# Image additions as accumulating transfers, norm sums in passes of their own, setup beside the first sample: a fused convolution, filter and scan kernel on one Trainium2 core

## The reference

```
h = x + conv3x3(relu(mask(groupnorm(x))))          # the mask depends on each channel's centre of mass
h = h + filter1(groupnorm(h))                      # 2x up by a 12-tap filter, leaky relu, clip, 2x down
g = groupnorm(h)                                   # input of the scan block
x', z = split(in_w @ g)                            # 1x1 convolution, 128 + 128 channels
f1, f2, f3 = 1x1 conv of x', then two 2x2 stride-2 convs   # levels of 784, 196 and 49 pixels
y  = selective scans with 16 states over f3, f2, f1 (both directions), layer norm of each, upsampled and added
h = h + out_w @ (y * silu(z))                      # x3 in the kernel
out = h + filter2(groupnorm(h))
```

## Time and profile before

| | |
|---|---|
| median of 3 runs | 6593.88 us (6589.45 to 6598.32) |
| profiled execution, its own time | 6592.31 us |
| its span, first to last instruction | 6590.5 us |
| PE busy | 5872.6 us (89%) |
| DVE busy | 5785.4 us (88%) |
| ACT busy | 4123.9 us (63%) |
| POOL busy | 269.1 us (4%) |
| mean granted TensorE clock | 0.935 of full |

### The profile page before, as it was taken

One profiled execution on the slowest core, in us unless ns is written; L12 is line 12 of the kernel. 1 busy time (PEld: TensorE's weight loads), 2 busy tenths in 40 slices (PEclk: granted clock), 3 DMA queues, 4 the chain that ended last, 5 costly groups with the idle time before them and its releaser, 6 DMA issues. The chain is left out here.

```text
span 6590.5 us, 87758 instructions
## 1 busy us (share of the span) xinstructions
PE 5872.6 (89%) x32460; PEld 3815.8 (58%) x32460; DVE 5785.4 (88%) x4685; ACT 4123.9 (63%) x8002; POOL 269.1 (4%) x69
## 2 busy tenths in 40 slices
PE   5779999999999999999999999999999989999956
PEld 3445656655656655656655656655556655666634
DVE  1798889989899988989989899989899989899984
ACT  2556666666666666666666666666666666676654
POOL 0000000000000000000000000000000000000000
PEclk9889999999999999999999999999999999999978
DMA  1333323333333333323333333333333333333331
GB/s 41 92 92 85 102 81 105 98 86 89 96 86 105 98 83 92 99 82 106 98 82 93 95 88 105 98 85 90 97 87 104 98 87 88 101 85 102 98 83 41
DMA packets 332919, 597.12 MB, mean 91 GB/s; under 512 B 105718, under 2 KB 174526, under 8 KB 332362
## 3 DMA queue, kind: packets, MB, share of 16 engines
q1 hardware_dynamic: 332492, 591.50, 33.9%
HBM read 294.91 MB, written 58.81 MB: 54 GB/s over the span
## 5 line engine op out<-in xcount | busy, mean ns | idle before, releaser
L1209 DVE TENSOR_TENSOR_SCAN hb<-da,hb 128x1570 f32<-128x1570 f32 (+2 forms) x704 | 2332.7, 3343 | 6.1 <-ACT da L1020 2.2
L641 PE MATMUL ps<-pad,conv_w 128*128 128x392 f32 x4608 | 1563.9, 493 | 0.0
L641 PEld LDWEIGHTS ps<-pad,conv_w 128*128 128x128 f32 x4608 | 870.2, 189 | 660.7 <-issue 42.7
L691 PEld LDWEIGHTS ps<-down_k,ys 121*128 121x128 f32 x9216 | 1108.2, 193 | 205.7 <-DVE ys L1085 120.5
L691 PE MATMUL ps<-down_k,ys 121*128 121x121 f32 (+1 forms) x9216 | 1137.7, 276 | 83.0 <-DVE ys L1085 82.9
L672 PE MATMUL ps<-xt,up_k 123*121 123x256 f32 (+2 forms) x4096 | 1149.2, 426 | 6.6 <-ACT ys L920 6.3
L1224 DVE TENSOR_TENSOR hb<-hb,c_t 128x3136 f32<-128x3136 f32 (+1 forms) x384 | 1150.0, 3008 | 1.3
L1025 ACT ACTIVATE da<-delta_t,a_neg 128x784 f32<-128x784 f32 x1024 | 912.8, 940 | 316.3 <-DVE hb L1209 312.9
L1192 DVE TENSOR_TENSOR hb<-dx_t,b_t 128x3136 f32<-128x3136 f32 x256 | 880.4, 3439 | 49.6 <-PE ps L778 47.0
L920 ACT ACTIVATE ys<-ps 121x512 f32<-121x512 f32 x1152 | 670.2, 590 | 376.1 <-PE ps L672 246.6
L672 PEld LDWEIGHTS ps<-xt,up_k 123*121 123x121 f32 x4096 | 660.5, 192 | 330.3 <-ACT ys L920 159.8
(11 more groups left out here) (136 smaller groups left out, 5771.1 us busy)
## 6 DMA issues: line engine op xcount, KB each, us to landing
dx_t<-vc SPq DMA_DIRECT2D x256, 392.0 KB, 6.4
b_t<-scr SPq DMA_DIRECT2D x256, 392.0 KB, 4.1
delta_t<-vd SPq DMA_DIRECT2D x256, 392.0 KB, 6.9
c_t<-scr SPq DMA_DIRECT2D x256, 392.0 KB, 4.3
xa<-in_x SPq DMA_DIRECT2D x32, 784.0 KB, 4.4
xs<-xa SPq DMA_DIRECT2D x32, 784.0 KB, 3.3
xb<-xs SPq DMA_DIRECT2D x32, 784.0 KB, 5.5
out<-xb SPq DMA_DIRECT2D x32, 784.0 KB, 7.8
```

The source lines that it names most:

```text
L641: mm = nc.tensor.matmul(ps[:, half, 0:HALF], conv_w[:, c, tap, m * P:(m + 1) * P], pad[:, c, r0:r0 + HH // 2, tap % 3:tap % 3 + WW], start ...
L691: mm = nc.tensor.matmul(img(ps[:, reg, 0:17 * WW])[:, h + h0:h + h1, w + w0:w + w1], ys[0:KP, y % NY, at + n * P:at + (n + 1) * P], down_k ...
L1209: nc.vector.tensor_tensor_scan(h, a, b, 0.0, ALU.mult, ALU.add).then_inc(scan_done, 1)
```

## The change

Both identity matmuls are gone. `ca` and `x3` write what PSUM holds plus the bias, and POOL then issues a transfer that adds the image to it in SBUF: `ax.m` adds the input image, read again from HBM, to `xa`; `ay.m` adds the spilled image to `xb`. The step `back` falls away. Since the copies no longer see the finished image, norms 2 and 1 get `gp` passes on ACT, in place, which wait for the transfers. The projections of the last two scan branches (`bc.2` and `bc.3`) become one matmul pair, with one copy and one write. The setup block is gone: the first image is loaded first of all, constants in two lists after it, and the products that build the filter matrices stand on DVE just ahead of the first `clip`. All five tables are new, and a sample's filter 2 and last scan steps stand up to one pass earlier.

```diff
@@ conv
-                    if n == 0:
-                        nc.tensor.matmul(ps[:, half, 0:HALF], ident[:, :], xa[:, m, half * HALF:(half + 1) * HALF], start=True, stop=False)
...
-                                              start=False, stop=(i == NC * TAPS - 1))
+                                              start=(i == 0), stop=(i == NC * TAPS - 1))
@@ bo
-                    pe.wait_ge(x_back, 16 * (s + 1))
                     for half in range(2):
-                        nc.tensor.matmul(out[:, half, 0:HALF], ident[:, :], xb[:, m, half * HALF:(half + 1) * HALF], start=True, stop=False)
...
@@ gp
-                    spare_free(s, k, c)
-                    nc.scalar.activation(spare(k, c), image(k, c), ACT.Identity, accum_out=gsum[k][:, 0, c:c + 1]).then_inc(gn_act[k], 1)
+                    if k == FIRST_GN:
+                        act.wait_ge(x_added[c], 16 * (s + 1))
+                    if k == LAST_GN:
+                        act.wait_ge(x2_added[c], 16 * (s + 1))
+                    out = image(k, c)
+                    if k == B_GN:
+                        spare_free(s, k, c)
+                        out = spare(k, c)
+                    nc.scalar.activation(out, image(k, c), ACT.Identity, accum_out=gsum[k][:, c:c + 1]).then_inc(gn_act[k], 1)
@@ ca
-                    nc.scalar.activation(xa[:, m, half * HALF:(half + 1) * HALF], ps[:, half, 0:HALF], ACT.Identity, bias=conv_b[:, m:m + 1],
-                                         accum_out=gsum[FIRST_GN][:, half, m:m + 1]).then_inc(conv_added, 1)
+                    nc.scalar.activation(xa[:, m, half * HALF:(half + 1) * HALF], ps[:, half, 0:HALF], ACT.Identity,
+                                         bias=conv_b[:, m:m + 1]).then_inc(conv_added, 1)
@@ gpsimd
+                def ax(s, m):
+                    pool.wait_ge(conv_added, 4 * s + 2 * m + 2)
+                    pool.dma_start(xa[:, m, :], sample(t["x"], s)[:, m, :], accum_op=ALU.add).then_inc(x_added[m], 16)
+                def ay(s, m):
+                    pool.wait_ge(x3_done, 2 * s + m + 1)
+                    pool.wait_ge(x_spilled, 16 * (s + 1))
+                    pool.dma_start(xb[:, m, :], xs[s][:, m, :], accum_op=ALU.add).then_inc(x2_added[m], 16)
@@ sync, ahead of the table
+                sp.dma_start(xa[:, :, :], sample(t["x"], 0)).then_inc(x_loaded, 16)
+                for dst, src in early:
+                    sp.dma_start(dst, src).then_inc(s_early, 16)
...
@@ clip
+                    if y == 0:
+                        weights()
@@ tables
-zm@1 zc@0
+zm@1 ax.0@0 ax.1@0 zc@0 ay.0@1 ay.1@1
```

More of the change, by code:

```diff
@@ L86 @@
+bl.6@2 cl.4@2 bl.7@2 cl.5@2 xl.3.3@2 xl.3.1@2 xl.3.2@2 xl.3.0@2 dl.3.1@2 dl.3.0@2 dl.3.2@2 dl.3.3@2 cl.6@2 bl.8@2
+cl.7@2 spill@1 load@0 bl.9@2 bcw.0@1 bcw.1@1 cl.9@2 cl.8@2 bcw.2@1 dl.0.2@1 bl.1@1 xl.0.2@1 bl.0@1 cl.0@1 dl.1.3@1
+cl.1@1 xl.1.3@1 bl.2@1
 """
 PE_ORDER = """
-gm2.3@1 red.9@2 f1@1 f2@1 f3@1 bc.0@1 gm1.1@3 bc.1@1 gm1.0@0 bc.2@1 var.2@2 gm2.0@0 bc.3@1 z@1 red.10@2 gm2.1@3
-turn.0.0.0@3 turn.0.0.1@3 red.11@2 v.0@1 turn.0.0.2@3 turn.0.0.3@3 v.1@1 turn.0.1.0@3 up.0.0.0@3 up.0.0.1@3 up.0.0.2@3
@@ L230, in build @@
         F = [f1, f2, f3]
-        gsum = [sb(f"gsum{i}", [P, 2, NC]) for i in range(4)]
+        gsum = [sb(f"gsum{i}", [P, NC]) for i in range(4)]
         gsq = [sb(f"gsq{i}", [P, NC]) for i in range(4)]
@@ L739, in bc_of @@
                     lev, w = BRANCH[q]
+                    rows = 2 * N_STATE * (2 if q == 2 else 1)
                     out = take("bc", s, q)
                     pe.wait_ge(f_copied, 3 * s + lev + 1)
+                    weights = bc_w[:, w:w + (2 if q == 2 else 1), :].rearrange("p w r -> p (w r)")
                     for half, n in halves(LEN[lev]):
-                        mm = nc.tensor.matmul(out[0:2 * N_STATE, half, 0:n], bc_w[:, w, :], F[lev][:, half * HALF:half * HALF + n], start=True, stop=True)
+                        mm = nc.tensor.matmul(out[0:rows, half, 0:n], weights, F[lev][:, half * HALF:half * HALF + n], start=True, stop=True)
                     mm.then_inc(slot_full, 1)
@@ L998, in bce @@
                         act.wait_ge(scr_written, 16 * i)
-                    nc.scalar.copy(wide(bcr[0:2 * N_STATE, :], n), wide_ps(slot[0:2 * N_STATE, :, :], n)).then_inc(bc_copied, 1)
+                    nc.scalar.copy(wide(bcr[0:rows, :], n), wide_ps(slot[0:rows, :, :], n)).then_inc(bc_copied, 1)
                 def da_of(s, u, *p):
@@ L1262, in _ @@
                       "mix": mix, "gate": gate}
+                constants()
                 for kind, s, a in program(DVE_ORDER):
```

288 lines of the change are left out of this document (147 added, 141 removed).

## The result

The changed kernel takes 6234.5 us (median of 4 runs, 6221.8 to 6246.7) beside 6591.7 us for the kernel before (6588.4 to 6598.3): ratio 0.9457, interval 0.9431 to 0.9483. It is faster by 5.4%. The profiled execution takes 6223.9 us, with a span of 6222.1 us.

What follows compares the result with a forecast made beforehand. Bound: no single engine, but PE and DVE handing work over in a 197.6 us period. Sum: 6592.3 - 28 x (197.6 - 190) - 41 - 10 - 25 = 6303, given as 6305 us; range 6220 to 6400, wider 6180 to 6510.

Steps and rivals of the forecast that it cites:

- the start: Up to the first image's mask: image loaded ahead of the large weights, first sum at 12 us, saving 41 us.
- the fill: From the first mask until the fourth image's: 10 us off for PE's lighter passes.
- the end: After the last mask: 31 us less DVE work up to the gate, +6 net after it, so -25 us.
- PE's savings: Per image on PE: identity matmuls 6.9 us and halved wide `bc` matmuls 2.6 us, together 9.5 us less work.
- The new wait: Between convolution and filter 1's first transpose: a chain of 14.3 us, adding 6 us to PE's idle time.
- D: Time of the 392 KB accumulating transfer ahead of filter 1: taken as 7 us, entering one to one above that.
- The other moves: PE idle per period: -5 for clips and filter 2's norm, +3 ahead of `f1`, about -2.5 for slot waits.
- No bound by itself: Kernel before: DVE 180.1 and PE 182.0 us of work per 197.6 us period, handing over in turn; neither alone bounds it.
- The new order hands over no better: Rival: new waits use up PE's saving, period 196 to 198, only the ends pay, 6516 or 6475 us; chance 0.17.
- DVE becomes the bound: Rival: D of 3 to 4 and clips covered, period 183 to 186, 6152 us; chance 0.12.
- Slow transfers: Rival: held-up accumulating transfers, D of 17 us, period some 203, 6660 us; slower than before; chance 0.11.
- The rule against the change: DVE and POOL hinder each other; the skill warns GpSimd-issued transfers can be starved of descriptors and advises another queue.

Runs made afterwards that it cites:

- the old order with the new setup: Kernel before with only the new setup and the merged B/C product; its order, identity matmuls and sums in the copies stay: 6457.8 us, ratio 0.9794.
- The delayed transfer: Changed kernel with a plain 392 KB device-memory transfer issued and waited for on POOL ahead of `ax.1`: 6369.2 us, ratio 0.9656.
- the new order with matmuls: Changed kernel with both additions as identity matmuls again, sum passes kept, the copy loaded back by SP: 6819.4 us, ratio 1.0339.
- the run meant to tell it: Changed kernel with half of the reductions over the states left out for the two finest branches: 6222.0 us, ratio 0.9437.
- the old order with the transfers: Before's order tables with new setup, merged product, both additions as accumulating transfers and separate sum passes: 6958.4 us, ratio 1.0553.

## Why the prediction was right, and where it was off

The forecast was 6305 us with 6180 to 6510; measured were 6234.5. Against the profiled execution the sum of 6303 was 79 us too high. Term by term: the period 187.7 and not 190 (-66), the start as predicted (-41), the fill +8.6 and not -10 (+19), the end -57 and not -25 (-32).

- **PE's savings, 9.5 us.** The total is near: work fell by 10.5 us, to 171.5 where 172.5 was predicted. Its parts came out otherwise. The convolution's identity matmuls cost 2.4 us when they were put back, not 3.4. The wide `bc` matmuls fell from 144.3 to 42.9 us in the 28 periods, 3.6 us each and not 2.6, because they also run at a higher clock: 505 ns for a matmul of 392 columns, where the same merged pair takes 872 ns in the old order with the new setup.
- **Work into time.** The sum adds PE's work and PE's idle time, and takes it that work taken off shortens the period. The runs do not bear that out: 8.8 us less work on PE gave no time, and the 2.4 us put back cost 0.7. The period fell by as much as PE's work did (10.0 and 10.5 us) while DVE, with its work unchanged, idled 10 us less, and that came from the order. That the sum still fits is partly luck.
- **The new wait, chain 14.3 us, PE idle +6.** The place is right, the reason for the waiting only in part. D was 7 in the sum and is 4.9 us for the half that counts. The stretch is 13.2 us at full clock and 15.0 in the mean; with D = 4.9 the sum's own terms give 12.2. What makes it longer is not the transfer but PE's queue: the group mean stood behind one reduction and the transposes behind another and `v`, both slower at half clock, which the sum had at nothing. PE idles 4.8 us in the mean and not 6.5, half of it inside the layer norm. The delayed transfer agrees with D entering one to one in size, 4.2 us for 3.6.
- **The other moves.** -5 for the clips and filter 2's norm is -5.3 by the waits (2.2 and 3.1 us gone). +3 ahead of `f1` is a wait of 3.3 us there now, where the waits of before have 22.7/28 = 0.8. -2.5 for the slot waits around `f1`, `f2` and `z` is -1.5 (80.6 us in 28 images, now 38.1), and waits of 3.4 us inside the layer norm, 2.3 of them in the stretch above, were not seen. PE's idle time is 16.1 us where the sum had 17. With the 0.5 us by which 189.5 was rounded up and 1.0 us less work, this makes the 2.3 us by which the period was off. The addition to `xb` is hidden as predicted: ACT waited for it four times in 64.
- **What the prediction left out on DVE.** The softplus wait, which it said nothing addresses, fell by 3.5 us per image, and it stays in the old order with the new setup (108.9 us), so this is the order's doing. Against it stand 2.8 us for the scan factors. The late `da.2` that was feared is not where they arise in the image above: ACT ends its first part at 4901.44, and DVE works without a gap until its scan at 4904.97, so it has the slack of about 3 us that was predicted.
- **The start** was exact at 41 us: the first mask is at 23.2.
- **The fill** failed in its step "10 us off for PE's lighter passes". The old order with the new setup needs 498 us from the first mask to the fourth, the changed kernel 512, and the new order with matmuls 534. That points at the new order, whose fill the prediction did not count; which step does it was not followed up.
- **The end.** The step on the work from mask to gate gave 31 us and measured 40.5. The one that failed is "+6 net" after the gate: it is -16.4 (60.5 us for 76.9). What shortens that last filter was not tested.
- **No bound by itself.** The reading that two engines hand work to each other holds: DVE relieved by 12.3 us gives 1.2, PE relieved by 8.8 gives nothing, both together (12.3 and 11.7) 2.5. But the pair does not set the time by itself either, since both idle more in that last kernel. In the convolution VectorE is the bound. What sets the time in the other stages, PE's work or the round of waits over ACT, stays open: the run meant to tell it took no time off PE.
- **The rivals.** "The new order hands over no better" is out at 187.7 us. "DVE becomes the bound" came nearer than its chance of 0.12 said, with 7.4 us of idle time left, but DVE's own relief hardly shortens the period. "Slow transfers" needed D = 17; the slowest of 128 took 11.3 us. By the sum's own terms the first rival's 6475 at a period of 196 is 6471.
- **The rule against the change.** The row's side is seen again: beside POOL's multiplication three scans took 11.70 us, and 10.05 without it. Hold-ups of descriptors by whole scans do not show: DVE works through the second half's transfers as well, and they land within 4.7 to 5.3 us. The slow ones into `xa`, up to 11.3, are the first halves, beside other transfers. The Trainium skill (DMA: Bandwidth & Descriptors, section Anatomy of one DMA) would have given 2.9 us (an estimate from the page), and the sum near 6200 by it; the measurement, 4.9 us where the transfer is alone, is 1.7 times that, and it decides. That 6200 lies nearer to the result than 6305 is no support for the 2.9, since PE hardly waited for the transfer.

What the prediction did not see is how the parts depend on each other. It gave the transfers credit for PE's 6.9 us. In the runs, with the steps where they were put, the transfers in the old order cost 500 us (6958 beside 6458), the new order with matmuls is 585 us above the changed kernel, and only the two together gain 223 us over the new setup alone. The first transfer adds little to that.

## What to carry to other kernels

Moving an addition off TensorE changes when its operands are needed, and that can be worth more than the matmul time: here the output projection could move in front of a store and a reload. A change of operations and the order written for it have to be priced together, for each alone, as placed here, was slower than neither. And where in-order engines hand over in turn, taking work off one did not pay in a stage where another engine was the bound, so look at the busy time stage by stage before removing anything.

## What the runs showed of the hardware

- **Matmuls into four different groups of 32 output rows run side by side.** The reduction's eight matmuls of 392 columns take 1.53 us (16 records), and with four of them left 1.51 us (8 records, below). The conv's matmuls of the same width take 6.11 us for nine, 0.68 us each, which would be 5.4 us for eight. That is why leaving half of them out gave nothing. The Trainium skill (TensorEngine Tiling (Array Packing), section Key Properties) says that different tiles of the array can execute matmuls in parallel; the trace agrees.

```profile
4994.24 1.51 PE L734 MATMUL ps<-hb,sel 128*32 128x392 f32 x8 [0.25 <-DVE hb L1258]
```

- **An accumulating transfer took longer than a plain one of the same queue and size.** Medians in the kernel with the delayed transfer:

```profile
xa<-in_x POOLq DMA_DIRECT2D x64, 392.0 KB, 5.2
...
junk<-in_x POOLq DMA_DIRECT2D x32, 392.0 KB, 3.3
```

  The 5.2 us mix the two halves; the second half, issued just behind the plain transfer, takes 4.9 us (4.8 to 5.2) for 3.3 (3.1 to 3.6). The plain one goes from device memory to device memory, so the 1.6 us between them hold that difference as well. The accumulating one's issue also takes POOL 0.88 us for 0.53.

- **The same accumulating transfer takes nearly twice as long beside others.** In the changed kernel the half that is issued while SP's transfers of `dx_t` and `delta_t` are under way lands after 8.8 us in the median, the half that is alone after 4.9. In the old order with the transfers the second half, issued at 4472.09 with two `delta_t` transfers under way, took 10.2 us, and at 4683.59, ahead of them, 5.2.

- **The granted clock fell behind waits of PE.** It was 0.97 in the changed kernel's 28 periods, 0.94 with fewer conv matmuls, and 0.91 in the old order with the transfers. There the same records took 9.5 us more per period. Where PE had waited 8 us (the rows of the kernel with fewer conv matmuls), the reduction behind the wait took 2.84 us at a granted clock of 0.50 (the level of 1.2 GHz, from 4898.70 to 4901.50), and the same kind 5 us later 1.54 at 1.00. So a wait on PE can cost more than its own length. It does not always: the same two waits ahead of filter 1 left the clock at 1.00 in the image at 3234.80 and at 0.79 in the one at 4918.28, and what decides that is not shown.
